# Values alone between pairs of scores, the other products of a batch in four stretches, two of them sharing a bank, and means subtracted where they are used

## The reference

```
mod = (silu(c) @ w_mod).reshape(16, 6, 1, 128)         # sa, ca, ga, sb, cb, gb
ga, gb = sign(g) * max(|g|, 0.25)                      # of each gate
h = layernorm(x) * (1 + ca) + sa
q, k, v = split(h @ W_qkv + b_qkv)                     # 16 heads of 8 channels
attn = softmax(q k^T) / sqrt(128)                      # per head, 256 x 256
x = x + ga * ((attn @ v) @ W_out + b_out)
h = layernorm(x) * (1 + cb) + sb
x = x + gb * (fp6_blocks(h) @ fp6_blocks(W_ffn)^T + b_ffn)
```

## Time and profile before

| what | us |
|---|---|
| median of 3 runs | 273.89 |
| the three runs | 272.79, 273.89, 275.31 |
| the profiled execution | 273.2 |
| its span, first to last instruction | 271.4 |
| busy: TensorE | 252.9 (93% of the span) |
| busy: VectorE | 233.0 (86%) |
| busy: ScalarE | 205.9 (76%) |
| busy: GpSimd | 185.3 (68%) |
| SP, all the time that it waited for maxT | 58.9, 17 times |

### The profile page before, as it was taken

One profiled execution on the slowest core, in us unless ns is written; L12 is line 12 of the kernel. 1 busy time (PEld: TensorE's weight loads), 2 busy tenths in 40 slices (PEclk: granted clock), 3 DMA queues, 4 the chain that ended last, 5 costly groups with the idle time before them and its releaser, 6 DMA issues.

```text
span 271.4 us, 7574 instructions
## 1 busy us (share of the span) xinstructions
PE 252.9 (93%) x2568; PEld 165.2 (61%) x2568; DVE 233.0 (86%) x597; ACT 205.9 (76%) x414; POOL 185.3 (68%) x384
## 2 busy tenths in 40 slices
PE   2679999999999999999999999999999999999952
PEld 2356666666676666666666666666667666565631
DVE  6579997999899999999999999999998889852264
ACT  5255787978797879797979888887978777777620
POOL 5814071869777878787878888797978655637550
PEclk9999999999999999999999999999999999999996
DMA  5465577364726555364637362627263630100000
GB/s 140 119 184 156 148 231 194 108 172 141 191 86 174 163 138 161 101 208 129 185 96 193 117 182 93 196 98 195 93 180 109 179 116 24 45 24 22 0 31 31
DMA packets 21654, 34.94 MB, mean 129 GB/s; under 512 B 3408, under 2 KB 17504, under 8 KB 19696
## 3 DMA queue, kind: packets, MB, share of 16 engines
q1 hardware_dynamic: 18688, 31.71, 40.1%
q10 hardware_dynamic: 2928, 2.75, 3.3%
HBM read 22.88 MB, written 9.99 MB: 121 GB/s over the span
## 4 chain that ended last, share of the span: by engine, by line
PE 78%; DVE 9%; issue 3%; DMA 3%; SPq 2%; ACTq 2%; POOL 1%; ACT 1%; POOLq 0%; DVEq 0%
PE ps_p L1026 26%; PE ps_o L1056 21%; PE ps_pre L1078 5%; PE ps_p L1041 5%; PE ps_post L1109 3%; DVE neg_max L837 3%; PE ps_o L1095 3%; PE ps_post L1123 3%; PE ps_pre L1085 2%; PE ps_p L1156 2%; PE ps_pre L1072 2%; PE ps_post L1117 2%; PE ps_pre L1065 2%; DMA q_rows<-maxT 1%; ACTq L393 1%
## 5 line engine op out<-in xcount | busy, mean ns | idle before, releaser
L837 DVE TENSOR_REDUCE neg_max<-ps_p 128x2 f32<-128x512 f32 x256 | 164.1, 681 | 10.5 <-PE ps_p L1026 9.0
L653 ACT ACTIVATE probs<-ps_p 128x512 f32<-128x512 f32 x256 | 139.3, 596 | 20.6 <-PE ps_p L1041 16.4
L1026 PE MATMUL ps_p<-k_rows,q_rows 62*128 62x256 f32 x512 | 97.9, 307 | 0.7 <-DVE neg_max L837 0.4
L1041 PE MATMUL ps_p<-q_rows,k_rows 64*128 64x256 f32 x512 | 98.1, 308 | 0.4 <-DMA q_rows<-maxT 0.4
L1026 PEld LDWEIGHTS ps_p<-k_rows,q_rows 62*128 62x128 f32 x512 | 69.2, 185 | 29.8 <-DVE neg_max L837 12.9
L1041 PEld LDWEIGHTS ps_p<-q_rows,k_rows 64*128 64x128 f32 x512 | 69.7, 185 | 4.7 <-ACT probs L653 2.3
L1056 PE MATMUL ps_o<-probs,v_aug 128*32 128x256 f32 x1024 | 68.5, 385 | 0.3 <-ACT probs L653 0.3
L1056 PEld LDWEIGHTS ps_o<-probs,v_aug 128*32 128x32 f32 x1024 | 26.7, 109 | 20.0 <-ACT probs L653 0.8
L499 POOL CAST max_parts<-neg_max 128x16 fp32r<-128x16 f32 x32 | 6.3, 197 | 40.1 <-DVE neg_max L837 40.1
L525 POOL TENSOR_TENSOR qk_parts<-qk_full_sb,qk_parts 128x256 fp32r<-128x256 f32 x28 | 20.4, 730 | 2.3
L1078 PE MATMUL ps_pre<-hT,wqk_sb 128*128 128x256 f32 x56 | 17.9, 402 | 1.8 <-ACT hT L623 1.0
(11 more groups left out here) (142 smaller groups left out, 360.1 us busy)
## 6 DMA issues: line engine op xcount, KB each, us to landing
q_rows<-q_dram SPq DMA_DIRECT2D x30, 256.0 KB
k_rows<-k_dram SPq DMA_DIRECT2D x60, 128.0 KB
modb<-mod_rows_dram SPq DMA_DIRECT2D x16, 256.0 KB, 3.7
q_dram<-qk_parts SPq DMA_DIRECT2D x28, 128.0 KB, 2.4
k_dram<-qk_parts SPq DMA_DIRECT2D x28, 128.0 KB, 2.4
out_dram<-out_sb SPq DMA_DIRECT2D x16, 128.0 KB, 1.8
x_all<-in_L_attn_x_dram ACTq DMA_DIRECT2D x6, 256.0 KB, 4.4
q_rows<-maxT SPq DMA_DIRECT2D x64, 8.0 KB
```

The costliest lines, as they stand in the source:

```text
L653: act.activation(probs[:, v % 2, u % 4, :], ps_p2[:, (16 * b + u) % P2_BANKS, :], ACT.Exp).then_inc(exp_done, 1)
L837: dve.tensor_reduce(neg_max[:, half, :, r, j], ps_p1[:, (16 * b + s) % P1_BANKS, :].rearrange("p (q k) -> p q k", q=QT), AX_X, ALU.max, ne ...
L1026: ins = pe.matmul(ps_p1[:, (16 * b + s) % P1_BANKS, t * T:(t + 1) * T], q_rows[64 * r:64 * r + ROWS1, slot, i, t * P:(t + 1) * P], k_rows[ ...
L1041: ins = pe.matmul(ps_p2[:, (16 * b + u) % P2_BANKS, t * T:(t + 1) * T], k_rows[64 * r:64 * r + ROWS2, slot, i, t * P:(t + 1) * P], q_rows[ ...
```

## The change

Nothing is computed otherwise, except that the negated means are no longer made: VectorE's instruction behind bn_aggr goes, and what centres subtracts the mean that bn_aggr wrote (`mv1` has two buffers for that).

On TensorE, values now stand alone behind the pairs s = 0, 6, 10 and 12. The other products stand behind 2: transpose_o of b - 1 and linear of b - 3 (before: b - 2, at 14 of the step before); 4: q and k of c, transpose_norm; 8: transpose_max of half 0, project_v, project_out; 14: transpose_hd of b - 2, transpose_x of c + 1 (before: at 0 of the next step), transpose_max of half 1. The second half of ps_pre's bank, `ps_pre_b`, takes transpose_x, k and v, so that q and k, and a transpose_max and its neighbour, are written in one stretch; since one bank is not read and written at once, ScalarE's readers wait until the later of the two products is there.

ScalarE reads accordingly: hdT of b - 3 at s = 0, hT at 2 (was 1), q at 5 (was 3), onT at 6 (was 5), k at 7 (was 5), maxT of half 0 at 9 (was 7), v at 10 (was 9). VectorE's `finish` of b - 3 is at s = 4 (was 0). GpSimd quantises before it makes the feed-forward weights. SP stores the output before it places the maxima of half 0. At the start, k of batch 2 is projected two heads later, and VectorE takes the statistics of batch 3 before the modulation rows instead of after them. The last batches keep the order they had.

The diff, cut to its core:

```diff
@@ -109,11 +109,9 @@
...
-        mv1 = sb("mv1", [P, QT, 2])
-        nm1 = sb("nm1", [P, 2, QT])
+        mv1 = sb("mv1", [P, 2, QT, 2])
...
-        minus_one = sb("minus_one", [P, QT])
...
@@ -173,7 +170,8 @@
...
-        ps_pre = ps("ps_pre", [P, 512])[:, 0:T]
+        ps_pre_bank = ps("ps_pre", [P, 512])
+        ps_pre, ps_pre_b = ps_pre_bank[:, 0:T], ps_pre_bank[:, T:2 * T]
...
@@ -327,8 +325,8 @@
...
-                ins = eng.tensor_scalar(xh2[:, n, :], x1[:, n, :], nm2[:, n:n + 1], rstd2[:, n:n + 1],
-                                        ALU.add, ALU.mult)
+                ins = eng.tensor_scalar(xh2[:, n, :], x1[:, n, :], mv2[:, n, 0:1], rstd2[:, n:n + 1],
+                                        ALU.subtract, ALU.mult)
...
@@ -457,10 +455,10 @@
                 c = b + 3
                 if has(b + 1):
                     load_modb(b + 1)
+                if has(b - 3):
+                    store(b - 3)
                 if has(b + 1):
                     place_max(b + 1, 0)
-                if has(b - 3):
-                    store(b - 3)
...
@@ -576,8 +573,8 @@
                 if b == 0:
                     pool.wait_ge(const_ready, 1)
                 if has(b - 2) and b - 2 != LAST:
+                    quantise(pool, b - 2)
                     ffn_weights(b - 2)
-                    quantise(pool, b - 2)
                     residual2(b - 2)
...
@@ -617,10 +614,10 @@
...
-            def save_hT(c):
...
+            def save_hT(c, src=ps_pre, *before):
+
+                wait(act, (xT_full, c + 1), (v_full, c - 2), *before)
+                act.activation(hT[:, c % 3, :], src, ACT.Identity, scale=scaleT[:, c:c + 1],
...
+            def save_qk(c, kind, full, saved, src=ps_pre):
...
-            def save_maxT(b, half):
-                wait(act, (maxT_full, 2 * b + half + 1), (max_placed[half], 32 * b))
+            def save_maxT(b, half, *before):
+                wait(act, (maxT_full, 2 * b + half + 1), (max_placed[half], 32 * b), *before)
                 act.activation(maxT[:, half, :], ps_pre[0:16, 0:T], ACT.Copy).then_inc(maxT_saved, 1)
 
...
@@ -691,6 +688,8 @@
                 for s in range(16):
                     if has(b):
                         exponentials(b, s)
+                    if s == 0 and has(b - 3) and b - 3 < LAST - 2:
+                        save(b - 3, hdT_full, f_full, hdT[:, :], ps_post[:, :], hdT_saved)
...
                     elif s == 1 and has(b - 1):
                         save(b - 1, pv_done, o_full, oT[:, :], ps_o[:, :], oT_saved, 4)
-                    if s == 1 and pre:
-                        save_hT(c)
-                    if s == 3 and pre:
-                        save_qk(c, 0, q_full, q_saved)
+                    if s == 2 and pre:
+                        save_hT(c, ps_pre_b, (maxT_full, 2 * b + 2))
+                    if s == 5 and pre:
+                        save_qk(c, 0, k_full, q_saved)
...
-                    elif s == (5 if in_steps(c) else 7) and has(b - 1) and b - 1 != LAST:
+                    elif s == (6 if in_steps(c) else 7) and has(b - 1) and b - 1 != LAST:
                         save(b - 1, onT_full, y_full, onT[:, :], ps_post[:, :], onT_saved)
-                    if s == 5 and pre:
-                        save_qk(c, 1, k_full, k_saved)
-                    if s == 7 and has(b + 1):
-                        save_maxT(b + 1, 0)
+                    if s == 7 and pre:
+                        save_qk(c, 1, k_full, k_saved, ps_pre_b)
+                    if s == 7 and b == -1:
+                        save_maxT(0, 0)
+                    if s == 9 and has(b + 1) and b >= 0:
+                        save_maxT(b + 1, 0, (v_full, b + 2))
...
                     if s == 2 and b % 2 == 0 and 0 <= b < NB - 6:
                         load_x(act, b + 6)
-                    if s == 9 and has(b + 1) and b >= 0:
-                        save_v(b + 1)
+                    if s == 10 and has(b + 1) and b >= 0:
+                        save_v(b + 1, ps_pre_b)
...
-                    elif s == 13 and has(b - 2) and b - 2 != LAST - 1:
+                    elif s == 13 and b - 2 == LAST - 2:
                         save(b - 2, hdT_full, f_full, hdT[:, :], ps_post[:, :], hdT_saved)
                     if s == 15 and has(b + 1):
                         save_maxT(b + 1, 1)
...
-            def finish_stats(mv, nm, ve, aggregated, value):
+            def finish_stats(mv, ve, aggregated, value):
 
                 wait(dve, (aggregated, value))
-                dve.tensor_tensor(nm[:, :], mv[:, :, 0], minus_one[:, :], ALU.mult)
                 return dve.tensor_tensor(ve[:, :], mv[:, :, 1], eps[:, :], ALU.add)
...
+                    ins = dve.bn_aggr(mv1[:, c % 2, n, :], st1[:, n, :])
                 ins.then_inc(aggregated1, 1)
-                finish_stats(mv1, nm1[:, c % 2], ve1[:, c % 2], aggregated1, c + 1).then_inc(stats1_ready, 1)
+                finish_stats(mv1[:, c % 2], ve1[:, c % 2], aggregated1, c + 1).then_inc(stats1_ready, 1)
...
@@ -813,6 +813,9 @@
             dve.wait_ge(dve_setup, n)
             dve.tensor_tensor(wblk(wf_d), wblk(wf_q), spread(wf_sc), ALU.mult).then_inc(wfd_ready, 1)
 
+            stats1(FIRST + 1)
+            aggregate1(FIRST + 1)
+
...
@@ -825,8 +828,6 @@
 
             first_low_part(1, 0)
             first_low_part(1, 1)
-            stats1(FIRST + 1)
-            aggregate1(FIRST + 1)
...
@@ -963,7 +964,7 @@
                     if s == 0 and b - 3 == LAST:
                         for t in range(QT):
                             finish_last(t)
-                    elif s == 0 and has(b - 3) and b - 3 != LAST - 1:
+                    elif s == (0 if b - 3 == LAST - 2 else 4) and has(b - 3) and b - 3 < LAST - 1:
                         finish(b - 3)
...
-            def transpose_x(c, *before):
+            def transpose_x(c, dst, *before):
...
-                    ins = pe.transpose(ps_pre[:, n * P:(n + 1) * P], xhat[:, c % 2, n, :], ident[:, :])
+                    ins = pe.transpose(dst[:, n * P:(n + 1) * P], xhat[:, c % 2, n, :], ident[:, :])
...
-                    if b == -2 and s == 12:
+                    if b == -2 and s == 14:
                         project_qk(FIRST, 1, k_full, ps_pre[:, :], (q_saved, 1))
                     if b < 0 and has1(b, s):
...
                     if s == 0 and has(b - 1):
                         values(b - 1, 3)
-                    if s == 0 and pre:
-                        transpose_x(c, (maxT_saved, 2 * (b + 1)), (v_saved, 1))
...
                             transpose_o_last(t)
                     elif s == 2 and has(b - 1):
                         transpose_o(b - 1)
-                    if s == 2 and pre:
-                        project_qk(c, 0, q_full, ps_pre[:, :])
+                    if s == 2 and has(b - 3) and b - 3 < LAST - 2:
+                        linear(b - 3)
                     if s == 4 and pre:
-                        project_qk(c, 1, k_full, ps_pre[:, :], (q_saved, c - FIRST + 1))
+                        project_qk(c, 0, q_full, ps_pre[:, :], (maxT_saved, 2 * (b + 1)))
+                        project_qk(c, 1, k_full, ps_pre_b)
...
@@ -1227,16 +1227,16 @@
                         transpose_norm(b - 1)
                     if s == 6 and has(b):
                         values(b, 0)
-                    if s == 6 and has(b + 1):
+                    if s == (6 if b == -1 else 8) and has(b + 1):
                         transpose_max(b + 1, 0, (k_saved, c - FIRST + 1) if in_steps(c) else (maxT_saved, 2 * (b + 1)))
+                    if s == 8 and has(b + 1) and b >= 0:
+                        project_v(b + 1, ps_pre_b)
                     if s == 8 and b - 1 == LAST:
                         for t in range(QT):
...
                     elif s == 8 and has(b - 1):
                         project_out(b - 1)
-                    if s == 8 and has(b + 1) and b >= 0:
-                        project_v(b + 1, ps_pre, (maxT_saved, 2 * (b + 1) + 1))
                     if s == 10 and has(b):
                         values(b, 1)
                     if s == 12 and has(b):
@@ -1244,14 +1244,16 @@
...
-                    elif s == 12 and has(b - 2) and b - 2 != LAST - 1:
+                    elif s == (12 if b - 2 == LAST - 2 else 14) and has(b - 2) and b - 2 < LAST - 1:
                         transpose_hd(b - 2)
+                    if s == 14 and in_steps(c + 1) and c + 1 > FIRST:
+                        transpose_x(c + 1, ps_pre_b, (v_saved, b + 2), (maxT_saved, 2 * (b + 1) + 1))
                     if s == 14 and has(b + 1):
                         transpose_max(b + 1, 1, (v_saved, b + 2), (maxT_saved, 2 * (b + 1) + 1))
...
-                    elif s == 14 and has(b - 2) and b - 2 != LAST - 1:
+                    elif s == 14 and b - 2 == LAST - 2:
                         linear(b - 2)
```

More of the change, by code:

```diff
@@ L149, in adaln_block @@
         mv2 = sb("mv2", [P, QT, 2])
-        nm2 = sb("nm2", [P, QT])
         ve2 = sb("ve2", [P, QT])
```

(27 more changed lines are left out.)

3 lines of the change are left out of this document (removed).

## The result

The changed kernel takes 291.59 us (median of 4 runs, 290.91 to 294.74) against 274.38 of the kernel before beside it: ratio **1.061** (1.054 to 1.068). Slower, as forecast, but by 17 us and not 5: the time lies 7.6 us above the range's end of 284. Single executions are up to 5% longer at a granted clock of 0.93 to 0.96 (of these four the one of 294.74); the ratios, and the medians of the experiments, leave them out.

A forecast was written before the change was run, and what follows sets the result against it. TensorE sets today's 14.23 us step; after the change a loop through SP's queue would, at 14.85. Over 13 turns +7.8, less 1.3 at the start and 0.9 at the end: +5.6 on 273.2, forecast 278.8 us, range 268 to 284.

The forecast's parts named there:

- the loop that I gave the weight to: Through SP's queue, from head 8 to the next batch's head 8: 14.85 us per batch, setting the step, +7.8 us.
- Subtracting a strided mean instead of adding a packed one costs nothing: same operation, same count.: Where the means are taken off in centring: subtracting at use was to add no time.
- transpose_norm waits 0.4 us, inside what TensorE has in hand; floor 13.95.: On TensorE, waiting for finish of b - 3: 0.4 us, within its slack against VectorE; step floor 13.95 us.
- GpSimd's residual2 also waits for this finish; the price is the idle time that it now has: On GpSimd, before the second split: the wait for finish costs its idle time there, 1.0 us.
- if TensorE instead waits at transpose_o or transpose_norm for longer than 0.5 us, the floor was wrong: Sign to look for in the profile after: such a wait on TensorE would refute the 13.95 us floor.
- my 2.0, 10.25 and 2.6: Terms of SP's loop in us: head 8's scores2 to placing half 0; queue to half 1's end; then to scores2.
- The landing.: From the end of placing half 1's maxima to head 8's scores2: taken as 2.6 us, called the weak term.
- TensorE saves 0.5 us a step.: Products other than values on TensorE: 4.1 us a step instead of 4.62, so TensorE needs 13.6 us.
- The other new wait, which I had at 0.2 us: On TensorE at transpose_o, for oT's copy, which now stands behind hdT's: some 0.2 us.
- VectorE −0.16 us.: Two negations go from VectorE: 0.16 us a step surely, at most 0.5.
- The ends, −2.2 us.: Start and end of the kernel: -1.3 us from scores one pair earlier, -0.9 from the last three steps.
- The first rival: SP's loop does not bind, its turn 13.3 us; steps of 13.95, 267.1 us, faster; chance 0.2.

The follow-up runs named there:

- e2: The kernel before with only the negations taken out and the means subtracted at use, old order; 275.69 us, ratio 1.006.
- e3: The kernel before, negations still made and their packed result the operand, but GpSimd's centrings subtract instead of add; one run, 281.55 us.
- e10: The kernel before with negated mean and variance plus epsilon made by one VectorE instruction, GpSimd still adding; 273.69 us, ratio 0.996.
- e1: The changed kernel with its new order, but negated means made by VectorE again and added by GpSimd; 284.12 us, ratio 1.034.
- e6: e1 with maxima of half 0 transposed, copied and placed as early as before, copies of k, v and onT moved too; 282.10 us, ratio 1.029.
- e9: e6 with the feed-forward part put back, finish at s = 0, and the output stored behind place_max again; 278.74 us, ratio 1.015.
- e12: e1 with the feed-forward part put back as in e9, but the output's store left ahead of place_max; 283.21 us, ratio 1.031.
- e8: The changed kernel run once more, unaltered, for a second profile; 291.46 us.
- e7: The kernel before with the start's two moves alone (k of batch 2 projected later, statistics of batch 3 earlier); 273.87 us, ratio 0.997.
- e11: e6 with negated mean and variance plus epsilon made by one VectorE instruction, as in e10; 276.70 us, ratio 1.007.
- e4: e1 with the maxima of half 0 placed by ScalarE's DMA queue behind its own copy instead of by SP; 287.83 us, ratio 1.048.

## Why the prediction was wrong

The sign was right, though the loop that I gave the weight to is not the one that sets the time; the size was wrong by a factor of three. By its own steps:

- **"Subtracting a strided mean instead of adding a packed one costs nothing: same operation, same count."** This step failed. I looked at the stride and the count and not at the operation: `subtract` then `mult` takes 0.80 us, `add` then `mult` 0.45 (e2, e3, e10). Taking the mean off in this way costs 1.7 us in the old order; in the new order it costs some 7 (changed kernel against e1), since both centrings lie on the loop of the changed kernel. The trace of before had no `subtract` on GpSimd, so this was an operation not shown, to be bounded from both sides like any other. A row to bound it by was near: GpSimd's operation with two tensors on 256 elements, 0.73 us, though even this lies below the 0.80 that came.
- **transpose_norm waits 0.4 us, inside what TensorE has in hand; floor 13.95.** This step failed too. The size of the wait was right, 0.4 us in e1 and e6 (0.78 in the changed kernel). What was wrong is that it lies inside the slack: I worked it out from the order of one engine, and in a closed loop there is no start of the step to count from. finish depends on amax, amax on GpSimd's h, and that on the step before. Without the subtraction this loop takes 15.14 (e6). It is undone by putting the feed-forward part back, finish at s = 0 with it (e9: 14.61). The same holds of "GpSimd's residual2 also waits for this finish; the price is the idle time that it now has": that wait is a link of the 15.8 us loop (195.89 to 196.03 above), and there is no such wait in e9. My text named the sign of this error ("if TensorE instead waits at transpose_o or transpose_norm for longer than 0.5 us, the floor was wrong"), and that is what came.
- **SP's loop, 14.85 a turn.** The mechanism is shown: e12 against e9, 4.5 us and the chain above, whose turn has 1.94 us from head 8 to the issue, 10.71 of queue and 2.97 from there to the next head 8. Over e12's 13 turns these three are 1.97, 10.12 and 2.69 on average, 14.78 in all (a turn whose head 8 isn't held is counted to its landing and 0.14 more): my 2.0, 10.25 and 2.6 were right. But the turns scatter from 13.8 to 15.8. One shorter than TensorE's own 14.5 gives nothing back and one longer is paid in full, so the 13 turns took 194.4 us, where 193.0 were forecast and the earlier trace rows have 185.3. And the loop does not set the changed kernel's time: head 8 is held in the first batches alone (by 1.31 and 0.66 us in e8). Three loops overlap, of about 14.8 us on average through SP, 15.1 through TensorE and transpose_norm (e6), and 15.8 through GpSimd, and the time is that of the longest, not the sum. With `add` a pair of centrings takes 0.89 us and not 1.59, so by an estimate the last loop would be 15.78 less 1.40, 14.4: the subtraction costs only the 0.6 us a step by which it lifts this loop above the second. Had only SP's loop been there, the answer would have been e12's 283, still inside my range.
- **The landing.** The Trainium skill, "DMA: Bandwidth & Descriptors", section "Anatomy of one DMA", gives about 2.0 us fixed and next to nothing for 8 KB. It gives this for a DMA that GpSimd issues, which my prediction left out; these are SP's. From the start of an issue to its landing e12's chain has 3.49 and 3.82 us, and its 13 turns 2.44 to 4.39 (to the last update of the semaphore), with lay_out's transfers ahead of it; the two turns behind them, which have no lay_out, have 1.88 and 1.91. So the traces agree with the page's figure for a DMA alone, and not for one in company, as in the earlier trace rows. What lay_out puts ahead is 1 MB (two DMAs of 256 KB and four of 128 KB by the profile's page), not the 768 KB of my text.
- **TensorE saves 0.5 us a step.** By start distances the other products take 1.03, 1.47, 1.15 and 0.70 us in the changed kernel without the wait, 4.35 against 4.62 before and 4.1 forecast: half of the gain is there. The miss is q and k with transpose_norm, 1.47 for 1.25. And the scores take up 0.1: where a stretch is now values alone, ScalarE has less time before the next one. e9, with no loop on it, has TensorE busy in 14.56 of 14.61 us, and the step is 0.4 longer than before. But that is no work of TensorE's: the scores at s = 4 take 1.27 us from start to start, for 0.73 before. From the timelines of TensorE and ScalarE:

```profile
150.68 0.38 PE L1028 MATMUL ps_p<-k_rows,q_rows 62*128 62x256 f32 x1
...
150.86 1.80 ACT L654 ACTIVATE probs<-ps_p 128x512 f32<-128x512 f32 x3
...
151.52 0.38 PE L1043 MATMUL ps_p<-q_rows,k_rows 64*128 64x256 f32 x1
...
151.95 1.13 PE L1080 MATMUL ps_pre<-hT,wqk_sb 128*128 128x256 f32 x4
```

scores2 of head 5, at 151.52, waits for the exponential of head 3, which ScalarE starts at 150.86, behind the copies of oT and hT; the stretch ahead, transpose_o alone in e9, lasts only 0.59 us and does not cover this. The other new wait, which I had at 0.2 us, is oT's copy ahead of transpose_o, 0.1. So e9 does not show what TensorE would need in the new order with nothing in its way, and neither does another run.
- **VectorE −0.16 us.** It shows 13.54 for 13.74.
- **The ends, −2.2 us.** The start's −1.3 is not there (e7), and the last stretch after head 0 of batch 15 became 0.7 longer instead of shorter, 28.41 us for 27.67. It goes with the feed-forward part's new place: e9 and e12, which put that back, have 27.66. Which wait it is I did not look for.

The first rival (the loop does not bind, 267) needed 13.95 steps and was never near: the shortest in the new order are 14.43 (e11). Of the 13 us between 278.8 and 291.6, the subtraction on the loop is some 7 (changed kernel against e1), the feed-forward part's new place beside SP's loop about 1 (e1 against e12, not clear of their noise), and 4.4 lie between e12 and the forecast: 1.4 in the 13 turns of SP's loop, the rest in the ends, which I had at −2.2 us and which became 1.0 longer.

## What to carry to other kernels

Before moving an instruction to another place in an engine's order, write down the whole cycle that it closes, across engines and across batches, and its length: a wait of 0.4 us by one engine's own order was a cycle of 15.1 us. Where several cycles have about the same length, undoing one alone brings almost nothing (e4, e6 and e12 all stayed 2.9% or more above); take them away in pairs to see them. A loop whose length scatters around the floor costs more than its mean says (e12). And a change of the ALU operation is a change of cost: an operation that the trace doesn't show gets a range, even where shape and count stay.

## What the runs showed of the hardware

- GpSimd's tensor_scalar on 128x128 fp32 takes 0.80 us with (subtract, mult) and 0.45 with (add, mult), with the scalar operand packed or at a stride of two elements (e2, e3, e10).
- VectorE's small instruction with two inputs in SBUF stands until GpSimd's running one ends: in e6 `nm`, 2 elements a partition, starts 0.64 us ahead of `ve` beside x_res, and 0.08 where it is alone. The Trainium skill, "SBUF — State Buffer", section "Who interferes with whom", says that such an instruction "contends with a GpSimd instruction that reads SBUF"; the trace agrees. Fewer such instructions behind bn_aggr (e11) was worth 0.7 us a step.
- An 8 KB DMA behind 1 MB of others in one queue lands 2.4 to 4.4 us after the start of its issue (13 turns of e12; 4.07 in the earlier trace rows); with none of them ahead, 1.9 (the two turns behind).
